# Stacked attention: one biased exponential per head, read from PSUM, in place of a subtraction pass and one exponential

## The chip, the cores and the metric
One Trainium2 chip, one of its cores. The metric is the device time of one execution, in microseconds (us), taken as the median of several runs.

## The reference, cut to what matters
Four layers, each an attention over a context and a feed-forward block, and a self-attention inside the last block. The input x is 64 sequences of 128 tokens of 128 numbers; the context has 120 keys per sequence; there are 16 heads of 8 numbers. Everything is float32. Each attention computes, per sequence and head,

```
scores = einsum('bhqd,bhkd->bhqk', Q, K) / sqrt(8)      # plus a mask in layers 2, 3 and the self-attention
attn   = softmax(scores, axis=-1)
out    = einsum('bhqk,bhkd->bhqd', attn, V)
```

The softmax is the part that the change touches: per query and head, subtract the largest score, take the exponential, and divide by the sum.

## The kernel before, in words
The kernel is written by hand in phases that follow one another: loading, then for each layer an attention phase (`attention_phase`) and a feed-forward phase. The attention phases are called a0, a1, a2, a3 and, for the self-attention, s3. In an operand's name of the profile the prefix is `a_` for a0 to a3 and `s_` for s3. a0 has another layout of heads (`hepos=True`); a1, a2, a3 and s3 are "packed" (`packed = not hepos`), and they are what the change concerns.

An attention phase walks over the 64 sequences in 16 groups of 4 (`NG`, `GB`). A packed group has 16 units (`S = GB * U`, U = 4): unit s is one sequence and one set of four heads. The keys of the four heads are laid side by side, each masked to its own head (`masked_keys`, line 348), so that one matrix multiplication gives the scores of 128 queries against 4 x 120 keys (4 x 128 in s3) in one PSUM bank. The float32 keys and queries are split in a high and a low part, which are stacked by DMAs (lines 398 and 404) for one pass of TensorE.

Each engine runs its own program, in order, and semaphores tie them together:

- TensorE, in unit s (`group`): `scores` of unit s (line 786, with a mask a second matmul, line 792), `turn` of unit s-2 (four transposes, line 801), `values` of unit s-4 (line 825), and every fourth unit `output` (line 839). In some units one projection of the next group is added (`slot_of`: keys, H, queries and values in units 0, 4, 7 or 8, and 13; in s3 H, keys, queries and values in units 1, 4, 8 and 13).
- VectorE, in unit s (`softmax_shift`): the maximum over each head (line 547, PSUM to `MX`), other work of that unit (`between`: reciprocal line 560, normalisation line 566, H of the next group line 151, statistics line 580, the residual sum line 575, in some phases an eviction), then the subtraction of the maximum (line 552, PSUM to SBUF tile `PR`).
- ScalarE, in unit s: the copy of the turned tile of unit s-2 (line 710, `PT`), the exponential of unit s in place in `PR` (line 704), and evictions of projections (lines 662 to 698).
- GpSimd: for the next group, the low part of the keys, one mask multiplication, the low part of the queries, and three more mask multiplications (`prepare`; lines 459 and 348). It does that in 15 of the 16 groups; before the first group it does a part of it, and VectorE two multiplications.
- SyncE issues the DMAs.

Buffers: two score banks (`SC`), two maxima (`MX`), two transpose banks (`TP`), four `PR` and four `PT`. `scores` of unit n waits for the subtraction of unit n-2 (`at_least(pe, sub_ready, n - 1)`, line 782), and `turn` of unit n waits for its exponential (`exp_ready`). The loops run over pairs of groups in hardware (`groups_loop`), the first and the last group or groups are written out.

Of the kernel before, what the change touches and what calls it, by code (L numbers as in the profile page):

```python
# [18 lines left out]
ALU = mybir.AluOpType  # L19
ACT = mybir.ActivationFunctionType  # L20
AX = mybir.AxisListType
# [22 lines left out]
def at_least(eng, sem, value):  # L44

    if isinstance(value, int) and value <= 0:
        return
    eng.wait_ge(sem, value)
# [185 lines left out]
def attention_phase(nc, R, I, name, wq, wk, wv, wo, bq=None, bk=None, bv=None, bo=None, hepos=False,  # L234
# [8 lines left out]
    packed = not hepos  # L243
# [5 lines left out]
    KN = P if own_keys else KC  # L249
# [5 lines left out]
    with ExitStack() as stack:  # L255
# [27 lines left out]
        PR = [sb(n_(f"p{i}"), [P, W]) for i in range(4)]  # L283
        PT = [sb(n_(f"pt{i}"), [P, 4 * P]) for i in range(4)]
        MX = [sb(n_(f"mx{i}"), [P, 16 if hepos else 4]) for i in range(2)]
        RD = sb(n_("rd"), [P, P])
        CT = [sb(n_(f"ct{i}"), [P, P]) for i in range(2)]
        SC = [ps(n_(f"sc{i}"), [P, 512]) for i in range(2)]
# [33 lines left out]
        sc_ready, mx_ready, sub_ready, exp_ready = (sem(n_(s)) for s in ("sc_ready", "mx_ready", "sub_ready", "exp_ready"))  # L322
        tp_ready, pt_ready, pv_done = (sem(n_(s)) for s in ("tp_ready", "pt_ready", "pv_done"))
# [34 lines left out]
        with nc.Block() as block:  # L358
# [117 lines left out]
            def _(dve):  # L476
                v = nc.vector
# [61 lines left out]
                def softmax_shift(g, s, between=()):  # L539

                    n = g * S + s
                    sc, mx = SC[s % 2], MX[s % 2]
                    k = KCLS if hepos else KN
                    heads = W // k
                    view = sc[:, 0:W].rearrange("p (h k) -> p h k", k=k)
                    dve.wait_ge(sc_ready, n + 1)
                    v.tensor_reduce(mx[:], view, AX.X, ALU.max).then_inc(mx_ready, 1)  # L547
                    for f in between:
                        f()
                    at_least(dve, tp_ready, n - 3)  # L550
                    dve.wait_ge(mx_ready, n + 1)
                    v.tensor_tensor(PR[s % 4][:].rearrange("p (h k) -> p h k", k=k), view,  # L552
                                    mx[:].unsqueeze(2).to_broadcast([P, heads, k]),
                                    ALU.subtract).then_inc(sub_ready, 1)
# [61 lines left out]
                def group(g, par, first, last):  # L616
                    for s in range(S):
                        work = work_at(g, s, par, first, last)
                        if U == 1 and s == 0 and not last:
                            ln_group(g + 1)  # L620
                        softmax_shift(g, s, () if U == 1 else work)
                        if U == 1:
                            for f in work:
                                f()
                    if last:
                        for u in range(S - RECIP, S):
                            if (u + 1) % U == 0:
                                of_sequence(reciprocals, g, u)
                                of_sequence(normalise, g, u)
                        add_out(g)  # L630
# [19 lines left out]
            def _(act):  # L650
                a = nc.scalar
# [49 lines left out]
                def exponentials(g, s):  # L701
                    n = g * S + s
                    act.wait_ge(sub_ready, n + 1)
                    a.activation(PR[s % 4][:], PR[s % 4][:], ACT.Exp).then_inc(exp_ready, 1)  # L704

                def turned(g, s):
# [5 lines left out]
                def group(g, par, first, last):  # L712
                    for s in range(S):
                        if not (first and s < TURN):
                            turned(g, s - TURN)
                        exponentials(g, s)
                        if not last:
                            for step in steps_of:
                                if slot_of[step] == s:
                                    evict(step, g + 1, 1 - par)  # L720
                                    if packed and step in "kq":
                                        high_part(step, g + 1)
                    if last:
                        for u in range(S - TURN, S):
                            turned(g, u)
# [13 lines left out]
            def _(pe):  # L739
# [32 lines left out]
                def scores(g, s, par):  # L772
                    n = g * S + s
                    j, i = s // U, s % U
                    if packed and j == 0:
                        pe.wait_ge(km_ready[i], g + 1)
                        pe.wait_ge(q3_in[i], 48 * (g + 1))
                    if hepos and s == 0:
                        for slot in range(4):
                            pe.wait_ge(km_ready[slot], g + 1)  # L780
                        pe.wait_ge(ready["q"], g + 1)
                    at_least(pe, sub_ready, n - 1)
                    masked = mask is not None or causal is not None or pad is not None
                    queries, keys = ((QR[par][:, i, j * P:(j + 1) * P], KM[par][:, i, j, :]) if packed else
                                     (QT[par][:, j * P:(j + 1) * P], KM[par][:, j, i, :]))
                    last = t.matmul(SC[s % 2][:, 0:W], queries, keys, start=True, stop=not masked)  # L786
                    if pad is not None:
                        b = g * GB + j
                        rows = padb[0:1, b, :].unsqueeze(1).to_broadcast([1, 4, KC])
                        last = t.matmul(SC[s % 2][:, 0:W], R.ones_bf[0:1, :], rows, start=False, stop=True)  # L790
                    elif masked:
                        last = t.matmul(SC[s % 2][:, 0:W], R.ident_bf[:],  # L792
                                        addm[:].unsqueeze(1).to_broadcast([P, 4, KN]), start=False, stop=True)
                    last.then_inc(sc_ready, 1)
# [58 lines left out]
                def group(g, par, first, last):  # L853
                    for s in range(S):
                        scores(g, s, par)
                        behind(g, s, par, first)
                        if not last:
                            for step in steps_of:
                                if slot_of[step] == s:
                                    project(step, g + 1, 1 - par)  # L860
                    if last:
                        for s in range(S, S + OUTPUT):
                            behind(g, s, par, False)
# [1366 lines left out]
```

## Time and profile before

| | us |
|---|---|
| median of 3 runs | 4307.19 (4302.86 to 4308.01) |
| the profiled execution | 4304.42 |
| its span, first to last instruction | 4302.6 |
| TensorE busy | 3552.4 (83%) |
| VectorE busy | 3327.7 (77%) |
| ScalarE busy | 2333.0 (54%) |
| GpSimd busy | 1642.7 (38%) |
| mean granted TensorE clock | 0.893 |

The span is cut at these places: the packed attentions are at work from about 578 to 1030 us (a1), 1400 to 1890 (a2), 2560 to 3042 (a3) and 3105 to 3637 (s3). In the rows PE is TensorE's matmul, PEld its weight load, DVE VectorE, ACT ScalarE, POOL GpSimd, SP SyncE; L547 is line 547 of the kernel. Shares are averages over phases with different limits. In a timeline several instructions of one kind that follow each other are merged into one row (xN), whose time is from the first start to the last end.

### The profile page before, as it was taken

What the parts mean: (1) busy time and instruction counts of PE and PEld (TensorE: products, weight loads), DVE (VectorE), ACT (ScalarE), POOL (GpSimd) and SP (SyncE); (2) the same over time, 40 slices, a digit from 0 to 9 for tenths busy, and PEclk for the clock granted to TensorE, in tenths of its full rate; (3) what the DMA queues carried; (4) which work ended last, traced back from release to release, by engine and by line L of the source; (5) the groups of instructions that cost most, each with busy time, mean ns of one, the idle gap of its engine ahead of it and who ended that gap; (6) DMA issues with size and microseconds to landing.
All of it is one profiled execution on the core that took longest, in us unless ns stands there. A gap on an engine that the chain in (4) does not pass through costs nothing. (4 is left out here: it accounts for less than half of the span.)

```text
span 4302.6 us, 95379 instructions
## 1 busy us (share of the span) xinstructions
PE 3552.4 (83%) x31830; PEld 2474.5 (58%) x31831; DVE 3327.7 (77%) x6125; ACT 2333.0 (54%) x4244; POOL 1642.7 (38%) x909
## 2 busy tenths in 40 slices
PE   6983979999598899982067749999499998799999
PEld 3552646667365566662045536666366666677777
DVE  7888879997897888883044458888788778788888
ACT  3432657775475566640044436767566665466665
POOL 2210045552000545433745555555155443222222
PEclk9985989997799999985588869999699999799999
DMA  1012022222000222212123342222222112100000
GB/s 62 16 35 96 0 63 63 66 63 68 1 0 11 66 56 59 56 62 61 51 48 50 50 89 60 60 59 57 58 54 53 46 46 67 40 15 15 15 15 15
DMA packets 172168, 200.65 MB, mean 47 GB/s; under 512 B 37692, under 2 KB 126080, under 8 KB 169793
## 3 DMA queue, kind: packets, MB, share of 16 engines
q1 hardware_dynamic: 149441, 181.01, 15.7%
q0 software_dynamic: 22528, 16.92, 2.9%
q8 instruction: 132, 2.16, 0.2%
q14 instruction: 67, 0.55, 0.0%
HBM read 48.90 MB, written 38.01 MB: 20 GB/s over the span
## 5 line engine op out<-in xcount | busy, mean ns | idle before, releaser
L704 ACT ACTIVATE a_p<-a_p 128x480 f32<-128x480 f32 x832 | 501.6, 603 | 517.4 <-DVE a_p L552 515.1
L348 POOL TENSOR_TENSOR a_km<-a_k,a_slots 96x1920 fp32r<-96x1920 f32 x186 | 631.8, 3417 | 179.9 <-DMA a_k<-a_kh 179.9
L547 DVE TENSOR_REDUCE a_mx<-a_sc 128x4 f32<-128x480 f32 (+1 forms) x832 | 542.2, 652 | 126.2 <-PE a_sc L792 96.5
L552 DVE TENSOR_TENSOR a_p<-a_sc,a_mx 128x480 f32<-128x480 f32 x832 | 531.2, 638 | 18.8
L710 ACT ACTIVATE a_pt<-a_tp 120x512 f32<-120x512 f32 x832 | 487.8, 586 | 82.9 <-PE a_tp L801 77.8
L801 PE MATMUL a_tp<-ident,a_p 128*120 128x128 f32 x3328 | 510.0, 276 | 4.1 <-ACT a_p L704 2.3
L801 PEld LDWEIGHTS a_tp<-ident,a_p 128*120 128x120 f32 x3328 | 400.0, 138 | 90.0 <-ACT a_p L704 27.1
L786 PE MATMUL a_sc<-a_km,a_qr 96*128 96x480 f32 x768 | 395.8, 515 | 33.6 <-DMA a_qr<-a_ql 29.5
L825 PE MATMUL a_nd<-a_pt,a_vm 120*32 120x128 f32 x6656 | 354.5, 285 | 0.0
L825 PE MATMUL a_nd<-a_pt,a_dm 120*32 120x128 f32 x6656 | 334.4, 273 | 0.0
L1760 ACT ACTIVATE f_s<-f_pu 128x512 f32<-128x512 f32 x256 | 153.5, 600 | 212.8 <-PE f_pv L1249 212.8
L1945 POOL DMA_INDIRECT summed<-f_yo,f_xr x128 | 202.5, 1582 | 153.2 <-ACT f_yo L2035 118.8
L547 DVE TENSOR_REDUCE s_mx<-s_sc 128x4 f32<-128x512 f32 x256 | 176.3, 689 | 97.4 <-PE s_sc L792 96.7
L2060 PE MATMUL f_px<-ident,f_xr 128*128 128x128 f32 x128 | 27.4, 353 | 271.5 <-DMA f_xr<-dispatched 271.5
L560 DVE RECIPROCAL a_rd<-a_nd 128x128 f32<-128x128 f32 x256 | 242.4, 947 | 6.7 <-PE a_nd L825 6.5
L348 POOL TENSOR_TENSOR s_km<-s_k,s_slots 96x2048 fp32r<-96x2048 f32 x62 | 224.0, 3633 | 52.2 <-DMA s_k<-s_kh 52.2
L1646 POOL TENSOR_TENSOR f_ya<-f_ya,f_yg 128x512 f32<-128x512 f32 x96 | 125.1, 1303 | 302.4 <-DVE f_yg L1696 302.3
L704 ACT ACTIVATE s_p<-s_p 128x512 f32<-128x512 f32 x256 | 161.1, 629 | 146.1 <-DVE s_p L552 144.6
L1671 DVE TENSOR_TENSOR f_a<-f_s,f_pv 128x512 f32<-128x512 f32 x256 | 175.2, 684 | 76.5 <-ACT f_s L1760 68.7
L1683 DVE TENSOR_TENSOR f_al<-f_a,f_ah 128x512 fp32r<-128x512 f32 x256 | 229.0, 895 | 0.0
L786 PEld LDWEIGHTS a_sc<-a_km,a_qr 96*128 96x128 f32 x768 | 146.4, 191 | 138.3 <-issue 130.1
L825 PEld LDWEIGHTS a_nd<-a_pt,a_vm 120*32 120x32 f32 x6656 | 131.2, 108 | 141.6 <-issue 132.2
(426 smaller groups left out, 8983.4 us busy)
## 6 DMA issues: line engine op xcount, KB each, us to landing
a_qr<-a_qh SPq DMA_DIRECT2D x384, 64.0 KB, 2.0
a_k<-a_kh SPq DMA_DIRECT2D x384, 60.0 KB, 2.0
a_ctx<-in_ctxT SPq DMA_DIRECT2D x64, 240.0 KB, 2.7
a_qr<-a_ql SPq DMA_DIRECT2D x192, 64.0 KB, 2.0
a_k<-a_kl SPq DMA_DIRECT2D x192, 60.0 KB, 2.0
dispatched<-f_empty SPq DMA_DIRECT2D x8, 1040.0 KB, 12.2
f_xr<-dispatched SPq DMA_DIRECT2D x32, 260.0 KB
s_k<-s_kh SPq DMA_DIRECT2D x128, 64.0 KB, 2.0
```

Source lines behind the costliest of these rows:

```text
L348: v.tensor_tensor(KM[par][:, i, :, :].rearrange("p b (j k) -> p b j k", k=KN), K3[:, i, :, :].unsqueeze(2).to_broadcast([TR, GB, 4, KN]), ...
L547: v.tensor_reduce(mx[:], view, AX.X, ALU.max).then_inc(mx_ready, 1)
L552: v.tensor_tensor(PR[s % 4][:].rearrange("p (h k) -> p h k", k=k), view, mx[:].unsqueeze(2).to_broadcast([P, heads, k]), ALU.subtract).the ...
L560: v.reciprocal(RD[:], ND[bt % 2][:, 1, :]).then_inc(rd_ready, 1)
L704: a.activation(PR[s % 4][:], PR[s % 4][:], ACT.Exp).then_inc(exp_ready, 1)
L710: a.activation(PT[s % 4][0:KN, :], TP[s % 2][0:KN, :], ACT.Copy).then_inc(pt_ready, 1)
L786: last = t.matmul(SC[s % 2][:, 0:W], queries, keys, start=True, stop=not masked)
L801: last = t.transpose(TP[s % 2][0:KN, q * P:(q + 1) * P], PR[s % 4][:, q * KN:(q + 1) * KN], R.ident[:])
L825: last = t.matmul(ND[j % 2][32 * q:32 * q + 32, what, :], w, PT[s % 4][0:KN, q * P:(q + 1) * P], start=(what == 0 and i == 0), stop=(i == ...
L1671: v.tensor_tensor(A[s % 2][:], S[s % 2][:], PV[s % 2][:], ALU.mult).then_inc(Z["a_ready"], 1)
L1683: v.tensor_tensor(AL[s % 4][:], A[s % 2][:], AH[s % 4][:].bitcast(F32), ALU.subtract).then_inc(Z["lo_ready"], 1)
L1945: nc.gpsimd.indirect_dma_start(out=R.summed[:, :], out_offset=bass.IndirectOffsetOnAxis(ap=XR[t % 4][:].bitcast(I32)[:, j, D + 1:D + 2], a ...
```

## The change
In the packed phases, VectorE no longer writes shifted scores. It takes the maximum as before, then negates it in place in `MX` (a `tensor_scalar` on 128 x 4 float32), and does its other work of the unit after that. ScalarE takes the exponential in four instructions, one per head, from the score bank in PSUM to `PR`, each with the head's negated maximum as the per-partition bias. The score bank and the maxima are therefore released by the exponential and not by the subtraction: TensorE's `scores` of unit n waits for `exp_ready` of unit n-2, and so does VectorE before it takes the maximum of unit n. The wait for a free `PR` moves from VectorE to ScalarE. a0 is unchanged.

```diff
@@ softmax_shift (VectorE)
                     dve.wait_ge(sc_ready, n + 1)
+                    if packed:
+                        at_least(dve, exp_ready, n - 1)
+                        v.tensor_reduce(mx[:], view, AX.X, ALU.max).then_inc(mx_ready, 1)
+                        dve.wait_ge(mx_ready, n + 1)
+                        v.tensor_scalar(mx[:], mx[:], -1.0, None, ALU.mult).then_inc(sub_ready, 1)
+                        for f in between:
+                            f()
+                        return
                     v.tensor_reduce(mx[:], view, AX.X, ALU.max).then_inc(mx_ready, 1)
@@ exponentials (ScalarE)
                     act.wait_ge(sub_ready, n + 1)
+                    if packed:
+                        at_least(act, tp_ready, n - 3)
+                        for j in range(4):
+                            ins = a.activation(PR[s % 4][:, j * KN:(j + 1) * KN], SC[s % 2][:, j * KN:(j + 1) * KN], ACT.Exp,
+                                               bias=MX[s % 2][:, j:j + 1])
+                        ins.then_inc(exp_ready, 1)
+                        return
                     a.activation(PR[s % 4][:], PR[s % 4][:], ACT.Exp).then_inc(exp_ready, 1)
@@ scores (TensorE)
-                    at_least(pe, sub_ready, n - 1)
+                    at_least(pe, exp_ready if packed else sub_ready, n - 1)
```

## Rows read from the trace of the kernel before
**Rows 1.** The page's busy time, share of the span and instructions.
```profile
PE 3552.4 (83%) x31830; PEld 2474.5 (58%) x31831; DVE 3327.7 (77%) x6125; ACT 2333.0 (54%) x4244; POOL 1642.7 (38%) x909
```
**Rows 2.** Windows in a1, a3, s3: length; busy PE, PEld, DVE, ACT, POOL; PEclk; DMA.
```profile
600.00:1000.00 400.00, 395.76 (x5174) 270.47 (x5173) 377.47 (x715) 286.15 (x528) 229.50 (x87) 1.00 0.26 63
2600.00:3000.00 400.00, 399.82 (x4984) 264.04 (x4982) 343.05 (x649) 280.87 (x505) 210.21 (x79) 1.00 0.24 59
3150.00:3600.00 450.00, 428.93 (x5020) 276.87 (x5018) 359.71 (x653) 291.11 (x507) 225.51 (x81) 0.95 0.21 50
```
**Rows 3.** Groups of instructions, whole span: busy us, mean ns, idle before.
```profile
L704 ACT ACTIVATE a_p<-a_p 128x480 f32<-128x480 f32 x832 | 501.6, 603 | 517.4 <-DVE a_p L552 515.1
L348 POOL TENSOR_TENSOR a_km<-a_k,a_slots 96x1920 fp32r<-96x1920 f32 x186 | 631.8, 3417 | 179.9 <-DMA a_k<-a_kh 179.9
L547 DVE TENSOR_REDUCE a_mx<-a_sc 128x4 f32<-128x480 f32 (+1 forms) x832 | 542.2, 652 | 126.2 <-PE a_sc L792 96.5
L552 DVE TENSOR_TENSOR a_p<-a_sc,a_mx 128x480 f32<-128x480 f32 x832 | 531.2, 638 | 18.8
```
**Rows 4.** GpSimd's timeline in a1: start us, us, instruction, [idle before].
```profile
807.20 1.21 POOL L459 TENSOR_TENSOR a_kl<-a_kt,a_kh 128x480 fp32r<-128x480 f32 x1 [4.76 <-ACT a_kh L662]
819.03 1.28 POOL L459 TENSOR_TENSOR a_ql<-a_qt,a_qh 128x512 fp32r<-128x512 f32 x1 [3.93 <-ACT a_qh L662]
820.27 10.08 POOL L348 TENSOR_TENSOR a_km<-a_k,a_slots 96x1920 fp32r<-96x1920 f32 x3
835.11 1.21 POOL L459 TENSOR_TENSOR a_kl<-a_kt,a_kh 128x480 fp32r<-128x480 f32 x1 [4.76 <-ACT a_kh L662]
```
**Rows 5.** s3: GpSimd's last run and TensorE's pause (timeline), a window after it.
```profile
3324.46 10.71 POOL L348 TENSOR_TENSOR s_km<-s_k,s_slots 96x2048 fp32r<-96x2048 f32 x3
3337.41 0.79 PE L786 MATMUL s_sc<-s_km,s_qr 96*128 96x512 f32 x1 [3.71 <-issue]
3337.40:3344.00 6.60, 6.59 (x49) 4.15 (x49) 4.53 (x10) 2.45 (x4) 0.00 (x0) 0.55 0.02 5
```
**Rows 6.** ScalarE's timeline: four small activations, and the next.
```profile
2299.76 1.14 ACT L2035 ACTIVATE f_yo<-f_po,f_xr 128x128 f32<-128x128 f32 x4 [0.45 <-PE f_po L2088]
2300.82 0.69 ACT L2022 ACTIVATE f_a<-f_pu,f_b 128x512 f32<-128x512 f32 x1
```
**Rows 7.** ScalarE's timeline in a3, back to back.
```profile
2717.04 0.60 ACT L704 ACTIVATE a_p<-a_p 128x480 f32<-128x480 f32 x1
2717.55 0.58 ACT L710 ACTIVATE a_pt<-a_tp 120x512 f32<-120x512 f32 x1
```
**Rows 8.** a3, timeline: two scores, a maximum, a subtraction under GpSimd's multiplication.
```profile
2717.86 0.47 PE L786 MATMUL a_sc<-a_km,a_qr 96*128 96x480 f32 x1
2719.49 0.48 PE L786 MATMUL a_sc<-a_km,a_qr 96*128 96x480 f32 x1
2720.23 0.66 DVE L547 TENSOR_REDUCE a_mx<-a_sc 128x4 f32<-128x480 f32 x1
2721.20 3.38 POOL L348 TENSOR_TENSOR a_km<-a_k,a_slots 96x1920 fp32r<-96x1920 f32 x1 [3.29 <-DMA a_k<-a_kh]
2721.67 0.59 DVE L552 TENSOR_TENSOR a_p<-a_sc,a_mx 128x480 f32<-128x480 f32 x1
```
**Rows 9.** A tensor_scalar with GpSimd at rest (timeline).
```profile
1903.49 0.19 DVE L125 TENSOR_SCALAR f2r_n_mean<-f2r_n_work 128x64 f32<-128x64 f32 x1
```
**Rows 10.** VectorE's tensor_scalars under GpSimd's instructions (timeline).
```profile
3078.55 3.60 POOL L440 MEMSET s_vm<- 128x2048 f32 x2
3079.12 1.29 DVE L125 TENSOR_SCALAR s_mean<-s_work 128x64 f32<-128x64 f32 x1
3080.72 1.47 DVE L130 TENSOR_SCALAR s_work<-s_work 128x64 f32<-128x64 f32 x1
3673.40 6.38 DVE L143 TENSOR_SCALAR f3r_h<-x,f3r_n_mean,f3r_n_rstd 128x128 f32<-128x128 f32 x8
3673.55 4.60 POOL L1020 TENSOR_TENSOR f_w2lo<-f3r_raw,f_w2hi 128x2048 fp32r<-128x2048 f32 x1 [3.09 <-DVE f_w2hi L1160]
```

## The prediction, made before the changed kernel ran
> **What bounds the kernel now.** I read the page's busy shares first: TensorE is busy for 83% of the span, VectorE 77%, ScalarE 54%, GpSimd 38% [rows 1]. These are averages over four stacked attentions (a1, a2, a3, s3) and other stages, and only the four are touched. So the second view is a table of windows inside them [rows 2]. In a1 TensorE is busy for 395.8 of 400 us and VectorE for 377.5; in a3 TensorE never rests (399.8 of 400) and ScalarE has 280.9, and a2 is like it; in s3 TensorE has 428.9 of 450 us. a1 is thus held by VectorE and TensorE together, a2 and a3 by TensorE.
>
> The groups of instructions give the softmax of a unit (one of 1024: 4 stages x 16 groups x 16 units) [rows 3]: maximum 652 ns, subtraction 638 ns, exponential 603 ns. The timeline of GpSimd gives the period of a group as the pitch from one low part of the keys (kl) to the next: 807.20 to 835.11, so 27.9 us in a1 [rows 4]. Each period holds kl 1.2, one mask multiplication 3.38 [rows 8], the low part of the queries (ql) 1.28 and three mask multiplications back to back, 10.08 us: GpSimd is at work for 16 of 27.9 us. In s3 the mask multiplications take 10.71 / 3 = 3.6 us each. There TensorE also stands for 3.7 us once in each pass of its loop (two groups), with no releaser that the profile shows ("issue"), and runs its next units at 1.2 GHz (0.55 granted over 3337.4 to 3344.0) [rows 5]. The last mask multiplication ended at 3335.17 and TensorE began at 3337.41, so GpSimd doesn't end this wait. The change leaves TensorE's program as it is, and I keep the stall in both times.
>
> **The change, part by part.**
>
> *VectorE loses the subtraction:* 1024 x 0.64 to 0.67 us, or 660 us of its work. That is on the path in a1 only, where it is nearly full.
>
> *ScalarE gets four exponentials for one.* No row shows an Exp of 120 columns with a bias. The nearest is L2035: 128 columns out of PSUM, a per-partition operand, four in a row: 1.14 us from first start to last end, and the next instruction starts 1.06 us after the first [rows 6]. Exponentials of today start 0.51 us before their successor [rows 7]. So the queue holds 1.06 instead of 0.51 us a unit: +0.55. Bounds: 0.51, if four quarters cost no more than the whole, and 4 x (0.265 + 0.08) = 1.4, the four without the overlap of 1.14 - 1.06 = 0.08 that rows 6 show. I take 1.06, same shape and count.
> ScalarE in a1 then has 16 x (0.50 + 1.06) = 25.0 us plus the evictions of keys, queries and H and two high parts, five activations of this size at 0.51 to 0.6 and a wait of a high part for its input: about 2.9; in all 27.9 us a group, an estimate from rows 7: just what a1's group takes [rows 4, 7]. No gain is left in a1; bubbles at the projections make it worse. I take +0.8 us a group there.
>
> *The scores wait for the exponential of two units before.* Unit pitch in a3 is 1.63 us (2717.86 to 2719.49), the maximum starts 0.74 us after the scores and lasts 0.66 [rows 8]. With about 0.2 for the negation and 1.14 for the exponentials a score tile is free at 0.74 + 0.66 + 0.2 + 1.14 = 2.75 us; it is wanted at 2 x 1.63 = 3.26. About 0.5 us of slack, so without other trouble nothing stops, except where the key and query evictions hold ScalarE (1.2 to 1.4 us in one unit). I take +0.3 us a group in a2 (its queries are evicted by VectorE), +0.6 in a3, +0.5 in s3. Bounds for this part: 0 (TensorE bound) and 1.4 + 1.2 = 2.6 us (both evictions unhidden).
>
> *VectorE gets the negation: this decides.* It is a `tensor_scalar` with an immediate, fp32, SBUF to SBUF, 4 elements. Alone it is cheap: L125 takes 0.19 us for 64 elements [rows 9]; I take 0.15. But such an instruction waits for GpSimd. When GpSimd clears a tile from 3078.55 to about 3080.35, L125 that starts at 3079.12 takes 1.29 us instead of 0.19 and ends just then; L130 under the second clear takes 1.47 us, to 3082.19. With a GpSimd tensor_tensor of 4.60 us, eight L143 of 128 elements take 6.38 us: the 4.60 and 8 x 0.22 for themselves [rows 10]. The subtraction, which reads PSUM, did not care: 0.59 us at 2721.67 inside a mask multiplication that runs from 2721.20 to 2724.58 [rows 8]. The pair of clears in rows 10 also shows that a waiting VectorE instruction slips in between two of GpSimd's.
> The Trainium skill says this in "SBUF — State Buffer", "Who interferes with whom": a one-source instruction in a two-port mode and a GpSimd instruction exclude each other for the whole instruction. By "VectorE: DVE Perf Modes", "Mode 2×_2P", four elements (an even count) qualify; no row here shows a four-element one, and by that rule the block happens every time.
>
> Price of the block. All behind it on VectorE waits too: the reciprocal, the statistics, the next maximum (0.65 us). That next unit's negation then arrives within the following multiplication, which already holds the port. So in a run of GpSimd instructions one unit passes for each.
> - Last run (ql and three multiplications): 1.28 + 10.08 + 0.3 for the negations between = 11.7 us, in which 3.75 units pass (a negation catches ql in 3 of 4 cases, since ql is 1.28 of a pitch of 1.6). They would take 3.75 x 1.56 + 0.1 = 6.0 us in a1 and 3.75 x 1.63 + 0.2 = 6.3 in a2 and a3. Lost: 5.7 and 5.4, less 0.5 of slack: 5.2 and 4.9.
> - The multiplication that stands alone: 3.38, less half a unit (0.8) before a negation meets it, less 0.5: 2.1.
> - kl: 0.2.
> - s3, with 3.60 for 3.38 and a unit pitch of 1.67: run 12.3 - 6.6 - 0.5 = 5.2, alone 2.3, kl 0.2.
> TensorE is ready again at once after a block, but a2 and a3 have no reserve to catch up with, and a1's new bound is ScalarE.
>
> **Sum per group:** a1 5.2 + 2.1 + 0.2 + 0.8 = 8.3; a2 4.9 + 2.1 + 0.2 + 0.3 = 7.5; a3 7.8; s3 5.2 + 2.3 + 0.2 + 0.5 = 8.2. Together 31.8. GpSimd prepares keys in 15 of 16 groups (186 multiplications in a1 to a3 [rows 3] = 3 x (15 x 4 + 2)): 31.8 x 15 = 477 us. The profiled execution took 4304.4 us (span 4302.6): 4781; the median of the three runs, 4307.2, is 3 us above it. I say 4780 us, 11% slower.
>
> **Rivals.**
> 1. *GpSimd isn't let go between its instructions.* Then a negation waits for the whole last run: 11.7 - 0.8 - 0.5 = 10.4 us instead of 5.0, +5.4 x 4 x 15 = 324: about 5105 us. Against it: L125 came through between two clears [rows 10].
> 2. *TensorE's clock falls in the runs.* TensorE would work 1.6 of 3.4 us. Pauses of 3.7 us brought 0.55 [rows 5]; here no pause is longer than about 2. If it falls, the units after the run go at 1.67 / 0.55 = 3.0 us instead of 1.67 for one or two units: +2 us a group, +120: 4900.
> 3. *The negation of four elements is not held back.* Then only the small terms stay: 0.8 + 0.3 + 0.6 + 0.5 = 2.2 us x 15 = 33: 4340.
> 4. *Faster.* The negation is free, and ScalarE runs without bubbles at the overlap of rows 7: 16 x (0.48 + 1.02) + 2.9 = 26.9 us a group in a1 for 27.9, since VectorE no longer binds there; 1.0 x 16 = 16 us gained, 0 in a2 and a3, where TensorE is full: 4291, -0.4%. It decides only if the four exponentials hold ScalarE for less than 1.06 us a unit, and never if rows 10 apply.
>
> **Chances.** Forecast 0.70, rival 1 0.07, rival 2 0.11, rival 3 0.09, rival 4 0.03. Within the forecast the units that pass in a run and the slack are the unknowns: 3 or 4.2 units for 3.75 and 0 or 1 us for 0.5 make 477 into about 330 to 610. The range 4500 to 4930 takes in rival 2 and most of that. Under 0.2% (9 us) a run can't be told from no change: faster 0.03, same 0.02 (part of rival 3), slower 0.95.
>
> **What would show it.** The negations: 1024 of about 0.15 us outside GpSimd's work, up to 3.4 us inside; mean over 1 us. Exponentials: x4096, four in 1.1 us. GpSimd's last run as long as now, with 4 units in it instead of 6. Pitch of kl: 36 us in a1, 38 in a2 and a3, 42 in s3, its stall still there. TensorE's share in a3 down to 80%. If the negations are short everywhere the step of rows 10 is wrong, and the time is near 4340; if one spans several multiplications, rival 1.

## The result, and the profile after

| | us |
|---|---|
| before, median | 4305.72 (4302.86 to 4308.01) |
| the changed kernel, median of 4 runs | 4731.37 (4725.40 to 4736.63) |
| ratio | 1.0989, 95% interval 1.0969 to 1.1008 |
| span of the changed kernel's profiled execution | 4734.8, mean granted clock 0.874 |

The change makes the kernel 9.9% slower. 4780 was forecast, within 4500 to 4930.

Busy shares of the changed kernel, to be laid beside [rows 1]:

```profile
PE 3706.8 (78%) x31830; PEld 2559.7 (54%) x31831; DVE 3528.5 (75%) x6125; ACT 2797.6 (59%) x7316; POOL 1642.9 (35%) x909
```

GpSimd's work is what it was. VectorE lost the subtraction and is busy for 201 us *more*: something that replaced 0.64 us costs more than it. The groups of instructions name it (busy us, mean ns, idle before; they answer to [rows 3]):

```profile
L715 ACT ACTIVATE a_p<-a_sc,a_mx 128x120 f32<-128x120 f32 x3072 | 866.6, 381 | 373.6 <-DVE a_mx L551 373.6
L551 DVE TENSOR_SCALAR a_mx<-a_mx 128x4 f32<-128x4 f32 x768 | 540.6, 704 | 26.5
L549 DVE TENSOR_REDUCE a_mx<-a_sc 128x4 f32<-128x480 f32 x768 | 495.5, 645 | 306.2 <-PE a_sc L807 240.5 <-PE a_sc L801 64.2
L801 PE MATMUL a_sc<-a_km,a_qr 96*128 96x480 f32 x768 | 416.8, 543 | 213.8 <-ACT a_p L715 179.8 <-DMA a_qr<-a_ql 30.7
L551 DVE TENSOR_SCALAR s_mx<-s_mx 128x4 f32<-128x4 f32 x256 | 191.6, 748 | 8.7
```

The negation of four numbers takes 704 ns on average, more than a maximum over 480 (645). ScalarE's exponentials idle for 373.6 us, all of it for the negation, and TensorE's scores for 213.8 us (33.6 before), 179.8 of them for the exponentials: the whole chain in three rows. A mean hides two populations. One run of GpSimd in a3 shows both. Timeline of GpSimd and VectorE, then TensorE's scores (start, duration):

```profile
2893.38 10.07 POOL L348 TENSOR_TENSOR a_km<-a_k,a_slots 96x1920 fp32r<-96x1920 f32 x3
...
2893.54 3.25 DVE L551 TENSOR_SCALAR a_mx<-a_mx 128x4 f32<-128x4 f32 x1
2896.70 0.28 DVE L574 TENSOR_TENSOR a_ct<-a_nd,a_rd 128x128 f32<-128x128 f32 x1
2896.90 0.64 DVE L549 TENSOR_REDUCE a_mx<-a_sc 128x4 f32<-128x480 f32 x1
2897.58 2.56 DVE L551 TENSOR_SCALAR a_mx<-a_mx 128x4 f32<-128x4 f32 x1
...
2900.92 2.56 DVE L551 TENSOR_SCALAR a_mx<-a_mx 128x4 f32<-128x4 f32 x1
...
2904.26 0.17 DVE L551 TENSOR_SCALAR a_mx<-a_mx 128x4 f32<-128x4 f32 x1
```
```profile
2893.71 0.48 PE L801 MATMUL a_sc<-a_km,a_qr 96*128 96x480 f32 x1
2897.99 0.48 PE L801 MATMUL a_sc<-a_km,a_qr 96*128 96x480 f32 x1 [0.47 <-ACT a_p L715]
2901.33 0.77 PE L801 MATMUL a_sc<-a_km,a_qr 96*128 96x480 f32 x1 [1.00 <-ACT a_p L715]
2904.68 0.77 PE L801 MATMUL a_sc<-a_km,a_qr 96*128 96x480 f32 x1 [0.29 <-ACT a_p L715]
2909.21 0.47 PE L801 MATMUL a_sc<-a_km,a_qr 96*128 96x480 f32 x1
```

Free, a negation takes 0.17 us; inside GpSimd's three multiplications it takes 2.56 to 3.25. A multiplication is a third of the 10.07 us, so the three end at about 2896.74, 2900.09 and 2903.45, and the held negations end at 2896.79, 2900.14 and 2903.48. The maximum (0.64) isn't held. Scores follow at 3.34 instead of 1.63 us: one unit for each multiplication. Two of the scores matmuls last 0.77 us instead of 0.48: TensorE has gone to half clock (the granted clock of this window is 0.50, or 1.2 GHz), of which more below.

```profile
2901.00:2909.00 8.00, 7.38 (x50) 4.89 (x51) 5.41 (x8) 4.99 (x17) 2.45 (x1) 0.50 0.07 18
```

Windows inside a1, a3 and s3 (length; busy PE, PEld, DVE, ACT, POOL; granted clock; DMA), to be laid beside [rows 2]:

```profile
620.00:1040.00 420.00, 363.19 (x4450) 249.73 (x4449) 365.93 (x618) 342.45 (x1052) 194.24 (x73) 0.95 0.21 53
2800.00:3300.00 500.00, 431.54 (x4541) 277.25 (x4540) 381.09 (x593) 343.39 (x1041) 194.27 (x73) 0.85 0.18 44
3550.00:4000.00 450.00, 383.90 (x4356) 244.06 (x4354) 351.32 (x565) 329.29 (x991) 200.53 (x71) 0.96 0.18 42
```

TensorE, without a rest in a3 before, is at 86% there, and its clock, 1.00 before, at 0.85. No engine is full any more. GpSimd's timeline gives the period of a group in a1, 34.05 us for the 27.91 of [rows 4]:

```profile
823.03 1.21 POOL L459 TENSOR_TENSOR a_kl<-a_kt,a_kh 128x480 fp32r<-128x480 f32 x1 [9.42 <-ACT a_kh L670]
...
837.74 10.07 POOL L348 TENSOR_TENSOR a_km<-a_k,a_slots 96x1920 fp32r<-96x1920 f32 x3
857.08 1.21 POOL L459 TENSOR_TENSOR a_kl<-a_kt,a_kh 128x480 fp32r<-128x480 f32 x1 [9.26 <-ACT a_kh L670]
```

The same pitch from kl to kl, meaned over the last 13 of each phase, is the measure of every experiment below (us a group):

| kernel | a1 | a2 | a3 | s3 | median |
|---|---|---|---|---|---|
| before | 27.92 | 30.48 | 30.16 | 33.86 | 4305.7 |
| changed | 34.12 | 36.86 | 41.24 | 38.74 | 4731.4 |
| negate in the maximum | 27.87 | 30.31 | 30.17 | 33.95 | 4300.5 |
| negation added alone | 37.28 | 43.29 | 43.35 | 41.30 | 4879.9 |
| halved multiplications | 28.87 | 32.91 | 31.90 | 35.74 | 4411.9 |
| four exponentials alone | 28.99 | 31.12 | 30.25 | 33.84 | 4334.1 |
| alternate units | 28.20 | 30.48 | 30.58 | 33.83 | 4317.7 |
| negation as a product | 34.16 | 36.85 | 40.94 | 38.38 | 4724.9 |
| filler in a3 | 34.12 | 36.63 | 40.96 | 38.28 | 4728.0 |
| before, s3 written out | 27.92 | 30.48 | 30.17 | 31.12 | 4270.0 |
| filler, a3 written out | 34.12 | 36.67 | 38.68 | 40.09 | 4719.2 |
| changed, s3 written out | 34.09 | 36.84 | 40.96 | 38.47 | 4727.6 |
| negate in the maximum, s3 written out | 27.90 | 30.32 | 30.17 | 30.93 | 4262.4 |

The negation added alone was profiled in a slower execution (4949.6 us; its others took 4852.3 to 4901.6), so its pitches are read as rough and its median as a little high.

The pitches account for the whole loss: 6.20 + 6.38 + 11.08 + 4.88 = 28.5 us more a group, x 15 = 428; the medians differ by 425.7.

### The profile page after: what moved, and what is told of

The parts are those of the page before. It is cut to its first block and busy times, and to the rows that moved or that the text cites. A ratio compares the mean times of both kernels' runs of the same rounds, so it can differ in the third digit from the quotient of the medians.

```text
span 4734.8 us, 99299 instructions
## 1 busy us (share of the span) xinstructions
PE 3706.8 (78%) x31830; PEld 2559.7 (54%) x31831; DVE 3528.5 (75%) x6125; ACT 2797.6 (59%) x7316; POOL 1642.9 (35%) x909
## 5 line engine op out<-in xcount | busy, mean ns | idle before, releaser
L715 ACT ACTIVATE a_p<-a_sc,a_mx 128x120 f32<-128x120 f32 x3072 | 866.6, 381 | 373.6 <-DVE a_mx L551 373.6
L549 DVE TENSOR_REDUCE a_mx<-a_sc 128x4 f32<-128x480 f32 x768 | 495.5, 645 | 306.2 <-PE a_sc L807 240.5
L801 PE MATMUL a_sc<-a_km,a_qr 96*128 96x480 f32 x768 | 416.8, 543 | 213.8 <-ACT a_p L715 179.8
L725 ACT ACTIVATE a_pt<-a_tp 120x512 f32<-120x512 f32 x832 | 512.1, 616 | 113.1 <-PE a_tp L816 105.7
L551 DVE TENSOR_SCALAR a_mx<-a_mx 128x4 f32<-128x4 f32 x768 | 540.6, 704 | 26.5
L816 PE MATMUL a_tp<-ident,a_p 128*120 128x128 f32 x3328 | 538.5, 287 | 0.0
L816 PEld LDWEIGHTS a_tp<-ident,a_p 128*120 128x120 f32 x3328 | 434.7, 145 | 78.6 <-issue 30.9
L715 ACT ACTIVATE s_p<-s_sc,s_mx 128x128 f32<-128x128 f32 x1024 | 298.5, 397 | 144.4 <-DVE s_mx L551 144.4
L840 PE MATMUL a_nd<-a_pt,a_vm 120*32 120x128 f32 x6656 | 369.6, 296 | 0.0
L840 PE MATMUL a_nd<-a_pt,a_dm 120*32 120x128 f32 x6656 | 350.1, 284 | 0.0
```

The lines of the kernel that those rows point to most:

```text
L551: v.tensor_scalar(mx[:], mx[:], -1.0, None, ALU.mult).then_inc(sub_ready, 1)
L715: ins = a.activation(PR[s % 4][:, j * KN:(j + 1) * KN], SC[s % 2][:, j * KN:(j + 1) * KN], ACT.Exp, bias=MX[s % 2][:, j:j + 1])
L725: a.activation(PT[s % 4][0:KN, :], TP[s % 2][0:KN, :], ACT.Copy).then_inc(pt_ready, 1)
L816: last = t.transpose(TP[s % 2][0:KN, q * P:(q + 1) * P], PR[s % 4][:, q * KN:(q + 1) * KN], R.ident[:])
L840: last = t.matmul(ND[j % 2][32 * q:32 * q + 32, what, :], w, PT[s % 4][0:KN, q * P:(q + 1) * P], start=(what == 0 and i == 0), stop=(i == ...
```

## The experiments

**Negate in the maximum.** The changed kernel without its negation: the reduction writes the negated maximum itself.

```diff
-v.tensor_reduce(mx[:], view, AX.X, ALU.max).then_inc(mx_ready, 1)
-dve.wait_ge(mx_ready, n + 1)
-v.tensor_scalar(mx[:], mx[:], -1.0, None, ALU.mult).then_inc(sub_ready, 1)
+v.tensor_reduce(mx[:], view, AX.X, ALU.max, negate=True).then_inc(sub_ready, 1)
```

> The changed kernel, but the maximum is written negated by the reduction itself (tensor_reduce with negate), so the tensor_scalar is gone; four biased exponentials and the longer hold of the score bank stay. Theory (the negation waits for GpSimd's port): 28 us a group go, and what stays are the small terms: 4305 to 4345 us, kl pitch near 28.5 us in a1, 30.5 to 31 in a2 and a3, 34 in s3, where the 3.7 us pause at the loop's turn comes back. Rival (the four exponentials and the score bank held until they end are what costs): the time stays within 50 us of 4731.

Measured: 4300.48 us, ratio to before 0.9986 (0.9976 to 0.9995). All of the 426 us are gone, and the time is just under the 4305 to 4345 expected. Its groups and its window in a1:

```profile
L549 DVE TENSOR_REDUCE a_mx<-a_sc 128x4 f32<-128x480 f32 x768 | 504.2, 656 | 513.1 <-PE a_sc L805 361.6 <-PE a_sc L799 143.8
L713 ACT ACTIVATE a_p<-a_sc,a_mx 128x120 f32<-128x120 f32 x3072 | 875.1, 398 | 33.4 <-DVE a_mx L549 32.6
```
```profile
620.00:1000.00 380.00, 372.10 (x4940) 260.62 (x4938) 245.00 (x464) 368.66 (x1161) 218.00 (x82) 1.00 0.25 62
```

The negating reduction costs nothing (656 ns; 652 before). VectorE falls from 94% to 64% of a1, and what takes its place is ScalarE, 97% busy: the group still takes 27.87 us, within 0.1 of the 27.9 that the forecast had summed for a full ScalarE. A third of VectorE's load in a1 was removed for 0.05 us a group.

**Negation added alone.** The kernel before, with a negation of the maximum ahead of the subtraction, which then adds.

```diff
+if packed:
+    dve.wait_ge(mx_ready, n + 1)
+    v.tensor_scalar(mx[:], mx[:], -1.0, None, ALU.mult).then_inc(neg_ready, 1)
-dve.wait_ge(mx_ready, n + 1)
+dve.wait_ge(neg_ready if packed else mx_ready, n + 1)
...
-                ALU.subtract).then_inc(sub_ready, 1)
+                ALU.add if packed else ALU.subtract).then_inc(sub_ready, 1)
```

> The kernel before, with the negation alone: maximum, negation in place by tensor_scalar, then the old pass as an addition and one exponential. Theory: the negation is held back by GpSimd here too, at one unit for each of GpSimd's instructions; there is more slack in a2 and a3 (about 1.0 us for 0.5) and none in a1, where VectorE is full: per group a1 +11, a2 and a3 +6, s3 +4; 4304 + 27 x 15 = 4710 us. Rival (the biased exponentials cost): VectorE only has 0.17 us more a unit, 2.7 us a group in a1 and nothing elsewhere: 4350 us.

Measured: 4879.86 us, 1.131 (1.1253 to 1.1366). The negation by itself costs more than the whole change.

```profile
L551 DVE TENSOR_SCALAR a_mx<-a_mx 128x4 f32<-128x4 f32 x768 | 494.2, 643 | 26.3
L556 DVE TENSOR_TENSOR a_p<-a_sc,a_mx 128x480 f32<-128x480 f32 x832 | 530.9, 638 | 19.5 <-DVE a_mx L551 0.9
```

The hold is there with one exponential and with the scores waiting for the subtraction as before. The size missed: 4710 was expected. VectorE's full load in a1 is not the reason: a1 lost 9.4 us a group, less than the 11 expected, while a2 and a3 lost 12.8 and 13.2 where 6 was expected. There TensorE's clock has fallen. Two groups of a2:

```profile
1594.97:1631.85 36.88, 32.77 (x386) 20.28 (x378) 35.88 (x68) 19.41 (x37) 15.91 (x6) 1.00 0.20 50
1669.73:1714.03 44.30, 38.25 (x379) 23.43 (x378) 39.22 (x68) 19.89 (x37) 15.90 (x7) 0.85 0.16 40
```

At clock 1.00 the group lost 6.4 us (36.88 for 30.48), as expected; at 0.85 it takes 44.30, and so do ten more behind it. The excess goes with the clock; whether the clock makes all of it is not shown.

**Halved multiplications.** The changed kernel, each of GpSimd's mask multiplications in two of half the size.

```diff
-    v.tensor_tensor(KM[par][:, i, :, :]..., K3[:, i, :, :]..., slots..., ALU.mult).then_inc(km_ready[i], 1)
+    for h, done in ((0, km_half[i]), (2, km_ready[i])):
+        v.tensor_tensor(KM[par][:, i, h:h + 2, :]..., K3[:, i, h:h + 2, :]..., slots..., ALU.mult).then_inc(done, 1)
```

> The changed kernel, with each of GpSimd's mask multiplications cut in two of half the size (1.7 to 1.8 us). Theory (one negation slips in between two GpSimd instructions): a run of 12 us now lets 7 units pass instead of 3.75, near the pitch of 1.6 us, so a group loses about 1.5 us in the run and 0.6 at the lone one: 4 x 2.1 + 2.2 = 10.6 x 15 = 160 us over before, 4465 us. Rival (what counts is how long GpSimd holds the port in all, not in what pieces): no change, 4731.

Measured: 4411.93 us, 1.0248 (1.0230 to 1.0265).

```profile
L350 POOL TENSOR_TENSOR a_km<-a_k,a_slots 96x960 fp32r<-96x960 f32 x372 | 658.8, 1800 | 177.2 <-DMA a_k<-a_kh 177.2
L554 DVE TENSOR_SCALAR a_mx<-a_mx 128x4 f32<-128x4 f32 x768 | 338.9, 441 | 26.5
```

GpSimd's multiplications take 4% longer in all (658.8 for 631.8 us), and three quarters of the loss are gone (4731 to 4412; 4465 was expected). The length of one instruction of GpSimd is the price, not the sum of them: the mean negation falls from 704 to 441 ns, and the longest hold from 3.42 to 1.81 us, since VectorE is let through at each boundary. A part of the gain is the clock's: a3's granted clock is back at 1.00.

**Negation as a product.** The changed kernel with `tensor_tensor(mx, mx, minus)`, `minus` a tile of -1.

```diff
-v.tensor_scalar(mx[:], mx[:], -1.0, None, ALU.mult).then_inc(sub_ready, 1)
+v.tensor_tensor(mx[:], mx[:], minus[:], ALU.mult).then_inc(sub_ready, 1)
```

> The changed kernel, with the negation written as a tensor_tensor product of the maxima and a tile of -1, both in SBUF. It tells whether only the tensor_scalar form waits for GpSimd. If every VectorE instruction that takes both read ports waits (GpSimd's multiplication reads SBUF too), the time is that of the changed kernel, 4731 within 20 us, and the products last up to 3.3 us. If only the tensor_scalar form does: 0.17 us each, and 4305 to 4315 us.

Measured: 4724.94 us, 1.0969 (1.0953 to 1.0986).

```profile
L554 DVE TENSOR_TENSOR a_mx<-a_mx,a_minus 128x4 f32<-128x4 f32 x768 | 534.0, 695 | 26.5
```

695 ns for 704: the same hold. An instruction with two inputs in SBUF waits like the one with an immediate, while the subtraction with one of its two in PSUM did not [rows 8]. The Trainium skill has this in "SBUF — State Buffer", "Who interferes with whom": two inputs in SBUF contend with a GpSimd instruction that reads SBUF. These numbers agree.

**Four exponentials alone.** The kernel before, its exponential in four, from `PR` and without bias.

```diff
+if packed:
+    for j in range(4):
+        ins = a.activation(PR[s % 4][:, j * KN:(j + 1) * KN], PR[s % 4][:, j * KN:(j + 1) * KN], ACT.Exp)
+    ins.then_inc(exp_ready, 1)
+    return
```

> The kernel before, with its exponential in PR cut in four by head, no bias, subtraction kept: what four instructions cost ScalarE, alone. Four of about 0.3 us in 0.85 us for 0.6. ScalarE has slack in all four stages, so 4305 to 4315 us. Rival (ScalarE's latency is already on the path): +0.3 us a unit in a1, 75 us.

Measured: 4334.12 us, 1.0063 (1.0046 to 1.0079). Its window in a1:

```profile
620.00:1000.00 380.00, 364.59 (x4726) 246.88 (x4723) 349.18 (x655) 316.70 (x1117) 207.18 (x79) 1.00 0.25 61
```

28 us more, a miss for both the 4305 to 4315 expected and the rival's 75 us: 1.07 in a1 and 0.64 in a2 a group, though neither VectorE (92%) nor ScalarE (83%) is full. TensorE's waits from 620 to 1000 us show where it goes (us in total, times, longest), first in the kernel before, then here:

```profile
PE a_tp L801 <- ACT a_p L704: 2.0, 13, 0.2
PE a_tp L806 <- ACT a_p L706: 15.1, 52, 0.4
```

The turn waits for the exponentials, 15.1 us in 13.1 groups for 2.0 in 13.6: 1.0 us more a group, which is the loss of a1.

**Alternate units.** Even units work as in the first experiment, with the negating maximum and the four biased exponentials; odd units work as before, with the subtraction and one exponential. The same condition is set at each place of the change; one of them is shown.

```diff
-if packed:
+if packed and s % 2 == 0:
```

> The kernel with the negated reduction and biased exponentials out of PSUM, but in even units only; odd units keep the subtraction and one exponential. Theory: in a1 the even form is held by ScalarE (97% busy, 27.9 us a group) and the old form by VectorE (27.9); half of each takes ScalarE to 16 x (0.50 + 0.79) + 2.9 = 23.5 us and VectorE below 80%, so TensorE binds: 16 x 1.43 + 4 x 0.21 + about 2.6 of projections = 26.4 to 26.8 us, 15 to 22 us off; a2, a3, s3 as they are, bound by TensorE: 4280 us. Rival (a1 is held by the latency of the chain, not by one engine's load): 27.5 to 28 us a group, 4300.

Measured: 4317.70 us, 1.0027 (1.0017 to 1.0037): a miss, 38 us over the 4280 expected. Balancing VectorE and ScalarE in a1 was to bring the gain that each alone kept back. The window in a1, and TensorE's waits in it:

```profile
620.00:1000.00 380.00, 366.88 (x4868) 255.22 (x4870) 296.07 (x565) 318.67 (x819) 216.22 (x82) 1.00 0.25 63
```
```profile
PE a_sc L799 <- ACT a_p L713: 11.0, 27, 0.5
```

VectorE at 78%, ScalarE at 84%, and the group takes 28.2 us for 27.9. With both at ease a1 is no faster, so VectorE's fullness before was no bound of its own. TensorE holds a1: in the kernel before it was busy for 376.05 of these 380 us and waited for 2.0. Here it is busy for 27.2 us a group (366.88 / 380 x 28.20), where the expectation had summed 26.4 to 26.8 for it, and it waits 0.8 us a group for the exponentials, the rival's part. The prediction's 'held by VectorE and TensorE together' fell in its first half. The rest of the 12 us lost to the kernel before is in a3, whose every second group takes 31.1 us.

**Before, s3 written out.** TensorE's program of s3 as 16 groups in line, no loop.

```diff
+if own_keys:
+    for g in range(NG):
+        group(g, g % 2, g == 0, g == NG - 1)
+    return
 groups_loop(pe, group, 3 if U == 1 else 1)
```

> The kernel before, with TensorE's loop over the groups of s3 written out, so that it never jumps back there. Theory (the 3.7 us pause in each second group is the jump back, waiting for instructions): all pitches in s3 near 31 us, 7 x 6 = 42 us off, 4263 us. Rival (the pause is something else of a pass, GpSimd's or the DMAs' cycle): the pause stays every second group, 4305.

Measured: 4270.04 us, 0.9919 (0.9904 to 0.9935). In the kernel before, groups of s3 are in turn:

```profile
3148.12:3179.24 31.12, 31.12 (x379) 20.17 (x378) 26.94 (x50) 21.61 (x39) 16.79 (x6) 1.00 0.22 53
3179.24:3215.99 36.75, 33.41 (x379) 21.57 (x378) 27.08 (x49) 22.16 (x39) 16.79 (x6) 0.91 0.19 46
```

Written out, all are at 31.1. The pause of [rows 5] is at the turn of TensorE's loop and costs, with the slow clock behind it, 5.6 us or more every second group. Why the turn takes so long is open.

**Filler in a3.** The changed kernel; in units 9 to 12 of a3, where GpSimd's run falls, TensorE does eight transposes of the identity that nobody reads.

```diff
+if name == "a3" and 9 <= s <= 12:
+    pe.wait_ge(ready["q"], g + 2)
+    for _ in range(8):
+        t.transpose(PJ[:, 0:P], R.ident[:], R.ident[:])
```

> The changed kernel, with eight transposes of the identity into the idle projection bank in units 9 to 12 of each group of a3 but the last: work for TensorE in the time in which it waits for the held negations, 1.1 us a unit at full clock. Theory (a3 loses 4 us a group more than a2 because TensorE's clock falls after it idled): the granted clock of a3 goes from 0.85 to over 0.95 and its pitch from 41.2 to 37 or 38, 45 to 60 us off, 4675 us. Rival (a3 is slow for where GpSimd's instructions meet its units, the low clock is only a sign): the filler is hidden or costs, 41 us or more, 4731 to 4760.

Measured: 4728.04 us, 1.0982 (1.0965 to 1.0999), no gain, where 4675 was expected. But the mean hid two kinds of group. Windows of one group each, from kl to kl, first in the changed kernel, then with the filler:

```profile
2875.38:2917.01 41.63, 36.26 (x377) 23.23 (x376) 31.36 (x50) 28.44 (x87) 15.90 (x6) 0.84 0.17 43
```
```profile
2905.25:2948.95 43.70, 36.58 (x392) 24.26 (x392) 31.12 (x49) 28.19 (x86) 15.90 (x6) 0.92 0.17 42
2948.95:2986.46 37.51, 35.19 (x426) 24.03 (x425) 30.21 (x51) 28.46 (x87) 15.90 (x7) 1.00 0.20 49
```

At clock 1.00 a group takes 37.5; the other kind holds this on TensorE:

```profile
2943.91 0.47 PE L801 MATMUL a_sc<-a_km,a_qr 96*128 96x480 f32 x1 [3.24 <-issue]
2946.41 1.34 PE L801 MATMUL a_sc<-a_km,a_qr 96*128 96x480 f32 x1
```

From 2800 to 3300 us the changed kernel has no such pause of TensorE, and this one has six, 20.2 us in all: a new wait that could have eaten the gain. Hence the next.

**Filler, a3 written out.** The filler, and a3's TensorE loop in line (the edit of s3, `name == "a3"`).

> The previous filler kernel with a3's TensorE loop written out, group by group, as well. In the filler kernel's a3 the groups at granted clock 1.00 have a pitch of 36.9 to 37.5 us, those at 0.89 to 0.92 one of 43.7 to 45.6, and the latter hold a pause of TensorE of 3.24 us that ends on "issue" once in each pass of the loop. Theory (the changed kernel's a3 is 4 us a group over its forecast because TensorE's clock falls; the filler cured that and its longer program brought the pause of the loop's turn, which took the gain back): all a3 groups at 1.00 and 37.1 us, 15 x (41.24 - 37.1) = 62 us under the changed kernel: about 4669. Rival (the pitch of 37 and 45 is an alternation of two halves of one pattern, and the clock follows from it): pitches still 37 and 45, time still about 4728. A weaker form of the first: pause gone, clock still falls after GpSimd's lone multiplication: about 39 us a group, 4700.

Measured: 4719.17 us, 1.0959 (1.0941 to 1.0978).

```profile
2908.58:2946.85 38.27, 34.36 (x409) 23.41 (x408) 31.53 (x50) 28.03 (x87) 15.90 (x6) 1.00 0.20 48
2946.85:2986.47 39.62, 35.73 (x409) 24.24 (x408) 31.36 (x50) 28.23 (x87) 15.90 (x6) 0.96 0.19 46
```

All groups of a3 at 38.2 to 39.7, none at 44: the pauses are gone and the weaker form holds (4700 was its time, 4669 the theory's). a3's mean is 38.68 for 41.24, 2.6 us a group or 38 us. The median fell by 12 only; in the profiled execution three groups of s3, untouched, take 45.4 to 45.7 us (s3 mean 40.09 for 38.74: 20 us given back). Why its loop pauses in that kernel and hardly in the changed one is open.

**Changed, s3 written out.** The edit of s3 on the changed kernel.

> The changed kernel with s3's TensorE loop written out. The pitches of its s3 are 38.3 us for most groups, without the 6 us alternation of the kernel before. Theory (the pause at the loop's turn is already hidden there by the waits for the exponentials, so the changed kernel gave back some 3 us a group that the forecast had kept in both): no change in the 38.3 us groups, only the three groups of 40.0, 42.7 and like ones may fall to 38.3: 4722 to 4731, at most 0.2% faster. Rival (the pause is still paid in some other form): 30 us or more faster, 4700, as the same edit brought 36 us to the kernel before.

Measured: 4727.58 us, 1.0977 (1.0959 to 1.0996); s3 at 38.47 for 38.74. What brought 36 us to the kernel before brings about 4 here, within the spread of the runs. The changed kernel pauses at that place once in s3 and seldom pays for it.

**Negate in the maximum, s3 written out.** Both edits that helped.

> Maximum and negation in one instruction (4300.48 us by itself) and s3's TensorE loop written out (4270.04 by itself, 4305.7 before). Theory: the two act in different places (a VectorE instruction less in a1 to s3; a pause of TensorE in s3 alone), so they add: 4300.5 - 35.7 = 4265 us, 0.94% faster than before. Rival: with ScalarE at 97% in a1 and the exponentials on the score bank's path, s3's tighter groups meet the exponentials and give part of it back: 4270 to 4285.

Measured: 4262.43 us, 0.9898 (0.9882 to 0.9915). They add: 1.0% faster than the kernel before, the fastest of all. s3's groups take 30.93 us. This is the version to keep, though most of it is not the change's doing.

## Why the prediction was right

The mechanism that was to decide, the held negation, is shown, and it makes the loss. That the total came within 49 us of 4780 is in part luck: three phases were priced too high and one too low.

*The block* was right in kind and place. A negation takes 0.17 us free (0.15 was said) and up to 3.4 us held. Removed, the loss goes (4300 us); alone, it is there (4880); with GpSimd's instructions halved, three quarters of it go (4412). *One unit passes for each multiplication*: the scores 3.34 us apart show it, and rival 1 (5105) is out. The mean negation of 0.72 us, (540.6 + 191.6) / 1024, is under the 'over 1 us' that was said: in a group four or five negations of 16 are held, and some only by the rest of an instruction.

*The price of a run and of the lone multiplication* was too high. Three of a2's last 13 groups are at clock 1.00, and this is one of them:

```profile
1689.65:1725.31 35.66, 31.14 (x378) 20.23 (x377) 30.45 (x52) 26.98 (x85) 15.91 (x6) 1.00 0.20 50
```

35.66 - 30.48 = 5.2 us, where 7.5 were forecast. Three negations are held in its run of 10.08 us (1.47, 2.56, 1.94 us): the first meets the first multiplication half way, and none meets ql, where the forecast had one caught by ql in three of four groups. a1, at clock 0.95 throughout, lost 6.2 for 8.3.

*The small terms*: 0.8, 0.3, 0.6 and 0.5 were said; with the negation folded into the maximum the four phases differ from before by -0.05, -0.17, 0.0 and +0.1. Together with the loss of the subtraction, the score bank's longer path and the bubbles of ScalarE cost nothing. *The four exponentials* take 1.11 to 1.12 us from first start to last end (1.14 was read off [rows 6]). ScalarE's sum of 27.9 us a group in a1 is near what it is busy there without the negation (97% of 27.87), but it is not what holds a1: with ScalarE at 84%, in the alternate units, a group takes 28.2.

*The clock*, rival 2, given 0.11, happened too, in a3 above all, where 11.1 us a group were lost for 7.8 forecast. The changed kernel's groups there are at 0.83 to 0.87 and take 40.6 to 41.6 us (one 43.9), but for one of 40.2 at 0.91; with the filler and the written-out loop, those at 1.00 take 38.3 at most, and the phase's mean is 2.6 us less. In a2 the groups at 0.95 take 37.1 to 37.5 for the 35.7 of those at 1.00. In s3 groups at 0.96 and at 1.00 both take 38.3, so there the clock costs nothing. What was held against rival 2, that no pause is longer than about 2 us, is true of a3 (1.9 us at most from 2800 to 3300) and did not keep the clock up. In the run shown above TensorE's pauses are 1.6 us and less,

```profile
2897.03 0.49 PE L854 MATMUL a_out<-a_wo,a_ct 128*128 128x128 f32 x2 [1.61 <-DVE a_ct L574]
```

and from 2901 on its matmuls take 0.77 us for 0.48.

*s3's pause* was kept in both times by the forecast, and it is all but gone in the changed kernel. TensorE's waits from 3480 to 3930 us, 12 groups of s3 (us in total, times, longest):

```profile
PE s_sc L801 <- ACT s_p L715: 51.1, 72, 1.9
PE s_sc L801 <- issue: 3.7, 1, 3.7
```

One pause instead of six, so s3 lost 4.9 us a group for 8.2. With the loop written out in both kernels it lost 38.47 - 31.12 = 7.4: the price of the block in s3 was nearly right, and the kept pause was the step that failed. Why the pause goes when TensorE waits for the exponentials is open.

So 31.8 us over the four phases were forecast and 28.5 measured. a1, a2 and s3 were 2.1, 1.1 and 3.3 us too dear, a3 with its clock 3.3 too cheap; without that last error the forecast would have been 6.5 us a group, or 98 us, too high instead of 49.

## What to carry to other kernels

Before a small VectorE instruction goes on the path of each unit, see what GpSimd does beside it: a tiny operation from SBUF to SBUF was priced here by the GpSimd instruction that it met, not by its four elements. First look for the form that folds it into its neighbour (here the reduction's own negation); if there is none, shorten GpSimd's instructions. And a mean pitch over groups hides a pause in every second one: read groups singly before a theory is dropped.

## What was not expected of the hardware

- TensorE's hardware loop pauses at its turn, 3.2 to 3.7 us with no releaser, in s3 before and in a3 with 32 more instructions a group, and seldom in the changed kernel. Written out in line, s3 alone gives 0.8%.
- A two-input instruction on four elements in SBUF is held as long as the one with an immediate (695 and 704 ns on average).
- TensorE's granted clock averages 0.85 in a3 of the changed kernel, with TensorE busy for 86% of 500 us and none of its waits longer than 1.9 us.
- A lower granted clock did not always cost time: in s3 of the changed kernel groups at 0.96 and at 1.00 both take 38.3 us, while a3's groups are 2.6 us shorter on average once the filler raises their clock.
